# Both layer normalisations of a pair as ScalarE activations, the second one a slot later, in a software-pipelined two-layer transformer kernel

## What is computed

```
x = x + tanh(g_xattn[0]) * attention_0(layernorm(x), ctx)      16 heads of 8
x = x + tanh(g_ffn[0])   * experts_0(layernorm(x))             8 experts, one per token
x = x + tanh(g_xattn[1]) * attention_1(layernorm(x), ctx)
x = x + tanh(g_ffn[1])   * experts_1(layernorm(x))             8 experts, two per token
layernorm(x) = (x - mean) / sqrt(var + 1e-5)
```

## Time and profile before

| | |
|---|---|
| median of 3 runs | 875.13 us (874.2 to 876.31) |
| the profiled execution | 874.29 us, its span 872.5 us |
| TensorE, share of the span busy | 536.8 us, 62% |
| VectorE | 484.0 us, 55% |
| ScalarE | 349.5 us, 40% |
| GpSimd | 285.4 us, 33% |

### The profile page before, as it was taken

The page is one execution under the profiler, slowest core; times in us unless marked ns, Lnnn a source line. Parts: engine busy times, 40 slices in busy tenths (PEclk is TensorE's granted clock), DMA queues, the critical chain, the costliest instruction groups (busy, mean ns, idle before and its releaser), DMA issues.

```text
span 872.5 us, 16776 instructions
## 1 busy us (share of the span) xinstructions
PE 536.8 (62%) x5459; PEld 427.9 (49%) x5459; DVE 484.0 (55%) x1521; ACT 349.5 (40%) x795; POOL 285.4 (33%) x342
## 2 busy tenths in 40 slices
PE   1688999987200008862798999861000199999960
PEld 0566666664100007651566667640000199999960
DVE  4668888874588203434789999847200034444324
ACT  1157777766100004321266777762000055555530
POOL 6102222201001754771011111010777435555550
PEclk9979999999555559995699999995555599999995
DMA  7543333320000312325455553200311212222219
GB/s 251 151 136 88 87 88 88 88 58 2 0 0 3 101 55 81 106 77 137 124 144 148 158 153 97 59 2 2 101 53 52 62 53 73 75 71 75 74 37 288
DMA packets 94628, 76.37 MB, mean 88 GB/s; under 512 B 13904, under 2 KB 88528, under 8 KB 94096
## 3 DMA queue, kind: packets, MB, share of 16 engines
q1 hardware_dynamic: 86432, 57.05, 24.0%
q0 software_dynamic: 7040, 14.53, 4.9%
q10 hardware_dynamic: 1072, 3.73, 1.3%
HBM read 45.54 MB, written 33.46 MB: 91 GB/s over the span
## 4 chain that ended last, share of the span: by engine, by line
PE 41%; POOL 15%; DVE 12%; issue 10%; DMA 9%; ACT 7%; SPq 4%; ACTq 1%; DVEq 0%; POOLq 0%
POOL dispatched L407 10%; PE bank L730 8%; PE bank L740 8%; PE bank L683 6%; PE bank L577 4%; PE bank L551 4%; POOL returned L414 4%; PE bank L565 4%; DMA QS_N<-MH 3%; DVE PT L979 2%; DVE MX L789 2%; ACT N L496 2%; DMA returned<-PT,META_ROW 2%; ACT PT L443 2%; PE bank L630 1%
## 5 line engine op out<-in xcount | busy, mean ns | idle before, releaser
L789 DVE TENSOR_REDUCE MX<-bank 128x4 f32<-128x512 f32 x256 | 172.9, 685 | 45.0 <-PE bank L577 44.8
L443 ACT ACTIVATE PT<-bank 128x512 f32<-128x512 f32 x256 | 152.7, 600 | 107.2 <-PE bank L565 106.4
L414 POOL DMA_INDIRECT returned<-PT,META_ROW x124 | 119.1, 961 | 111.8 <-DVE PT L1070 87.1
L521 ACT ACTIVATE XGT<-bank 128x256 f32<-128x256 f32 x62 | 23.8, 384 | 260.3 <-PE bank L551 260.3
L551 PE MATMUL bank<-CONST,PT 128*128 128x128 f32 x124 | 25.9, 292 | 148.2 <-issue 142.1
L577 PE MATMUL bank<-KS,QS_N 96*128 96x128 f16 x1024 | 104.8, 229 | 12.1 <-DMA KS<-spread 10.0
L565 PE MATMUL bank<-QS_N,KS 98*128 98x512 f16 x256 | 99.2, 391 | 8.2 <-DMA QS_N<-MH 7.8
L740 PEld LDWEIGHTS bank<-WALL,HT 128*128 128x128 f32 x808 | 98.8, 192 | 10.2 <-issue 7.0
L740 PE MATMUL bank<-WALL,HT 128*128 x808 | 101.1, 276 | 3.9 <-issue 1.5
L730 PE MATMUL bank<-XGT,XT_HL_WR 128*128 128x256 f32 x404 | 100.7, 389 | 0.0
L577 PEld LDWEIGHTS bank<-KS,QS_N 96*128 96x128 f16 x1024 | 78.5, 104 | 34.1 <-DMA KS<-spread 11.6
(11 more groups left out here) (172 smaller groups left out, 830.5 us busy)
## 6 DMA issues: line engine op xcount, KB each, us to landing
spread<-XT_HL_WR SPq DMA_DIRECT2D x128, 64.0 KB, 2.1
PT<-dispatched SPq DMA_DIRECT2D x62, 130.0 KB, 2.1
QS_N<-spread SPq DMA_DIRECT2D x128, 48.0 KB
KS<-spread SPq DMA_DIRECT2D x32, 192.0 KB
WALL<-in_w SPq DMA_DIRECT2D x8, 578.0 KB, 4.0
CT<-in_ctx SPq DMA_DIRECT2D x32, 128.0 KB, 2.7
spread<-XT_HL_WR SPq DMA_DIRECT2D x32, 128.0 KB, 2.3
dispatched<-in_pads SPq DMA_DIRECT2D x2, 1040.0 KB, 5.7
```

The source lines that it names most:

```text
L414: pool.indirect_dma_start(ys[layer][:, :], bass.IndirectOffsetOnAxis(ap=META_ROW[:, a.f, c:c + 1], axis=0), YS[:, a.f, c, :], None).then_i ...
L443: nc.scalar.activation(PT[:, c, 4 * g:4 * g + 4, :].rearrange("p j q -> p (j q)"), ST[i % 2][:, :], ACT.Exp, scale=SCALE[layer]).then_inc( ...
L789: V.tensor_reduce(out=MX[:, m.u, 2 * J * g + c:2 * J * (g + 1):2], in_=MB[i % 2][:, :].rearrange("p (j k) -> p j k", j=J), op=ALU.max, axi ...
```

## The change

- The second normalisation of a pair (z, now y) and all that follows it move one slot later for ScalarE and TensorE: N is made at the start of ScalarE's slot, behind exponential 4 of b; its transposes stand in TensorE's group 2; NT is copied behind exponential 7 of b; the logits go to PF in place of PA in group 4; LG is copied behind exponential 1 of a.
- The first normalisation XN becomes two ScalarE activations with a scale and an offset, behind exponential 1 of a, in place of two VectorE instructions between maxima 6 and 7.
- The small terms (variance plus epsilon, minus the mean) leave VectorE. GpSimd makes them, for both normalisations: three instructions more for n, two more for z. GpSimd takes z after the bias of n.
- VectorE's slot is put in another order. Behind maximum 0: MH as before; behind 1: reciprocal and OK of z (before: at the slot's end, for b); behind 2: statistics of n; behind 5: the new x of z (before: 3); behind 6: the low half of f (before: 5); behind 7: statistics of z (before: 4).
- TensorE's slot: the transpose of the maxima comes before score block 4; XN's transposes move from group 1 to 0; the first half of the weighted sums from 0 to 1, the second from 4 to 5; OK's transposes from 0 to 2; Wo and the logits from 2 to 4; the value projection from 5 to 6; OT's transposes from 6 to 7; N's transposes from 7 to the next slot's 2.
- On ScalarE, XT goes from behind exponential 6 to behind 5, and OKT from behind 5 to behind 6.

```diff
@@ GpSimd, attention_slot
-                        nc.gpsimd.tensor_tensor(out=RSTD[:, n.u, :], in0=VE[:, n.u, :], in1=EXPO[:, :], op=ALU.pow).then_inc(x_rstd, 1)
...
+                        chain.link(nc.gpsimd.tensor_scalar(out=VE[:, n.u, :], in0=MV[:, n.u, :, 1], scalar1=LN_EPS, scalar2=None, op0=ALU.add))
+                        nc.gpsimd.tensor_scalar(out=MINUS_X[:, n.u, :], in0=MV[:, n.u, :, 0], scalar1=-1.0, scalar2=None, op0=ALU.mult)
+                        chain.link(nc.gpsimd.tensor_tensor(out=RSTD[:, n.u, :], in0=VE[:, n.u, :], in1=EXPO[:, :], op=ALU.pow))
+                        nc.gpsimd.tensor_tensor(out=OFFSET[:, n.u, :], in0=MINUS_X[:, n.u, :], in1=RSTD[:, n.u, :],
+                                                op=ALU.mult).then_inc(x_rstd, 1)
...
+                        nc.gpsimd.tensor_scalar(out=MINUS[:, z.u, :], in0=MV_N[:, z.u, :, 0], scalar1=-1.0, scalar2=None, op0=ALU.mult)
+                        chain.link(nc.gpsimd.tensor_scalar(out=VE_N[:, z.u, :], in0=MV_N[:, z.u, :, 1], scalar1=LN_EPS, scalar2=None, op0=ALU.add))
@@ ScalarE, attention_slot
                     exponentials(b, 4)
                     if y:
...
+                        act.wait_ge(n_rstd, y.g + 1)
+                        for c in range(2):
+                            last = nc.scalar.activation(N[:, y.b + c, 0:D], batch(y, c), ACT.Identity,
+                                                        scale=RSTD_N[:, y.u, c:c + 1], bias=OFFSET_N[:, y.u, c:c + 1])
+                        last.then_inc(n_copied, 1)
 
                     exponentials(b, 5)
+                    if f:
+                        act.wait_ge(front_t, f.g + 1)
+                        nc.scalar.activation(XT[:, f.u, :], PF[:, 0:256], ACT.Copy).then_inc(front_kept, 1)
...
                     exponentials(a, 1)
...
+                    if n:
+                        act.wait_ge(x_rstd, n.g + 1)
+                        act.wait_ge(front_t, before(n.g - 1))
+                        for c in range(2):
+                            last = nc.scalar.activation(XN[:, n.u, c * D:(c + 1) * D], batch(n, c), ACT.Identity,
+                                                        scale=RSTD[:, n.u, c:c + 1], bias=OFFSET[:, n.u, c:c + 1])
+                        last.then_inc(x_norm, 1)
@@ TensorE, attention_slot, group 2
+                    scores_for_maxima(2)
+                    scores(b, 6)
                     if z and layer == 0:
                         pe.wait_ge(o_kept, z.g + 1)
                         for c in range(2):
                             last = transpose(PO[:, c * P:(c + 1) * P], OK[:, c * D:(c + 1) * D])
                         last.then_inc(ok_t, 1)
...
+                    if y:
+                        pe.wait_ge(n_copied, y.g + 1)
                         if m:
                             pe.wait_ge(v_kept, m.g + 1)
...
+                        if f:
+                            pe.wait_ge(front_kept, f.g + 1)
+                        pe.wait_ge(lg_kept, y.g)
                         for c in range(2):
...
+                            last = transpose(PF[:, 256 + c * P:256 + (c + 1) * P], N[:, y.b + c, 0:D])
+                        last.then_inc(n_t, 1)
@@ VectorE, attention_slot
                     maxima(7)
...
+                    if z:
+                        dve.wait_ge(x_new, z.g + 1)
+                        dve.wait_ge(n_stats, z.g)
+                        dve.wait_ge(n_copied, before(z.g - 1))
+                        stats(z, STATS_N, MV_N[:, z.u]).then_inc(n_stats, 1)
```

More of the change, by code:

```diff
@@ L491, in slot @@
                                              ACT.Copy).then_inc(v_kept, 1)
[L493 to L498, removed]
                     exponentials(a, 3)
@@ L582, in slot @@
                     scores_for_maxima(0)
-                    scores(b, 4)
                     if a:
@@ L594, in slot @@
                         last.then_inc(ok_t, 1)
[L596 to L599, removed]
+                    if y:
+                        pe.wait_ge(n_copied, y.g + 1)
                         if m:
                             pe.wait_ge(v_kept, m.g + 1)
-                        if y:
-                            pe.wait_ge(n_kept, y.g + 1)
+                        if f:
+                            pe.wait_ge(front_kept, f.g + 1)
+                        pe.wait_ge(lg_kept, y.g)
                         for c in range(2):
[L605 to L621, removed]
+                            last = transpose(PF[:, 256 + c * P:256 + (c + 1) * P], N[:, y.b + c, 0:D])
+                        last.then_inc(n_t, 1)
                     scores_for_maxima(3)
@@ L635, in slot @@
                     scores(a, 0)
-                    if b:
+                    if z and layer == 0:
+                        pe.wait_ge(ok_kept, z.g + 1)
+                        for c in range(2):
+                            last = nc.tensor.matmul(PO[:, 256 + c * P:256 + (c + 1) * P], OKT[:, c * P:(c + 1) * P],
+                                                    WSQ[:, 3, :], start=True, stop=True)
+                        last.then_inc(wo_done, 1)
+                    if y:
+                        pe.wait_ge(n_kept, y.g + 1)
+                        for c in range(2):
+                            last = nc.tensor.matmul(PF[:, 256 + E * c:256 + E * c + E], NT[:, c * P:(c + 1) * P],
+                                                    WG[:, layer, :], start=True, stop=True)
+                        last.then_inc(lg_done, 1)
+                    scores_for_maxima(5)
+                    scores(a, 1)
+                    if b:
+                        values(b, 1)
+                    scores_for_maxima(6)
+                    scores(a, 2)
+                    if r:
+                        pe.wait_ge(front_kept, f.g + 1 if f else r.g + 1)
                         if y:
                             pe.wait_ge(lg_kept, y.g + 1)
-                        values(b, 1)
-                    scores_for_maxima(5)
-                    scores(a, 1)
-                    if r:
-                        pe.wait_ge(front_kept, f.g + 1 if f else r.g + 1)
                         pe.wait_ge(v_kept, r.g)
```

100 lines of the change are left out of this document (40 added, 60 removed).

## The result

| | before | after |
|---|---|---|
| median | 875.14 us (874.2 to 876.31, 4 runs) | 885.95 us (883.71 to 886.67, 4 runs) |
| profiled execution | 874.29 us, span 872.5 | 886.01 us, span 883.9 |

The account below looks back on a forecast made before the run. A ring of waits, no full engine, was taken to bound the kernel. Full slots -0.6 and +2.9, draining -2.1, -1.5, -1.9, -1.4, tail +0.4, filling -1.65 summed to -5.85 us: 869 predicted, range 861 to 881.

Parts of the forecast that it names:

- the ring: Loop from maximum 7 through statistics, GpSimd, N, XT, TensorE and back sets the slot: 10.77 us layer 0, 10.14 layer 1.
- its sign in layer 1: Layer 1's full slots get longer, 10.14 us against 9.85, adding 2.9 us over ten slots.
- signs of being wrong: Prediction fails if small GpSimd instructions cost over 0.5 us, TensorE stops elsewhere, or layer 1's slot is under 9.85 us.
- x: Unknown price of the two new small GpSimd instructions before the power of z, between 0.10 and 1.38 us.
- With x = 0.30: Path from the start of maximum 7 to N's transposes takes 4.55 us, with the small GpSimd pair at 0.30.
- x = 0.65: Alternative price of the GpSimd pair at twice VectorE's 0.16 us each; whole 7 us slower, about 876.
- TensorE wakes 0.05: TensorE starts N's transposes 0.05 us after ScalarE's XT copy ends.
- the ends: Filling and draining of the layers' pipelines make -8.55 us of the sum, its roughest part.
- Draining: Slots without pair f get shorter: -2.1 and -1.5 us; each layer's last two slots another -1.9 and -1.4.
- Filling: First XN 0.75 us later in layer 0; three slots without y gain some 0.4 us each per layer: -1.65.
- GpSimd makes it slower: Small pair before the power of z costs more; every 0.1 us adds 2 us over 20 slots; chance 0.22.
- the ends give little: Filling and draining bring a third of their -8.55 us; about 875, no change; chance 0.17.

Follow-up runs that it names:

- e6_xn_on_dve: Changed kernel with the first normalisation XN back on VectorE as two instructions behind maximum 4; ratio to the kernel before 1.0127, layer 0 slot 11.12 us.
- e1: Changed kernel with ScalarE's XT copy ahead of N instead of behind N and exponential 5; ratio to the kernel before 0.9909, layer 0 slot 10.24 us.
- e2: Changed kernel with VectorE's statistics of z right behind the new x instead of behind maximum 7; ratio to the kernel before 0.9862, layer 0 slot 10.04 us.
- e4: Changed kernel with the second normalisation's two small instructions ahead of the power back on VectorE; ratio to the kernel before 0.9998, layer 0 slot 10.78 us.
- e5: Changed kernel with two more small chained GpSimd instructions ahead of the power of z; ratio to the kernel before 1.0681, layer 0 slot 11.72 or 13.37 us.
- e7: Changed kernel with one semaphore wait instead of four before TensorE's transposes of N; ratio to the kernel before 1.0058, layer 0 slot 10.94 us.
- e8_filler: Changed kernel with two groups of two throwaway TensorE matmuls in the draining slots of both layers; ratio to the kernel before 1.0137, layer 1 drain 39.95 us.
- e12_filler_l1: Changed kernel with throwaway TensorE matmuls in layer 1's draining slots alone; ratio to the kernel before 1.0077, layer 1 drain 39.96 us.
- e14_both_terms: Changed kernel with z's small pair back on VectorE and one wait before N's transposes; ratio to the kernel before 0.9963, layer 0 slot 10.61 us.
- b0: The kernel before, unedited, profiled again on a chip of the experiments; layer 0 slot 10.85 us, layer 1 drain 38.88 us.
- e0: The changed kernel, unedited, run again as control; ratio to the kernel before 1.0096, layer 0 slot 11.12 us, layer 1 drain 42.19 us.

## Why the prediction was wrong

**Right: the ring, its members and its sign in layer 1.** ScalarE idle about 1 us before N, released by OFFSET_N (1.18); TensorE stopped by XT and by maximum 7, and no stop for OKT or OT; XN covered on ScalarE (e6_xn_on_dve). e1, e2, e4, e5 and e7 each changed one member, and the slot of layer 0 followed within 0.1 us where the clock stayed up. One of my signs of being wrong did appear, a stop of TensorE elsewhere (0.35 us for OK), but it doesn't set the slot.

**Wrong by size: x.** The step "With x = 0.30": the pair costs 0.51 us (0.59 less one wake of 0.08), since the second one starts 0.29 us behind the first and the power 0.30 behind that. It neither overlaps fully nor costs a power. This is 0.21 us of a slot. My estimate of x = 0.65 by the Trainium skill, GPSIMD Engine Reference, section 4.1, misread it: the factor of about two is stated there for two-input operations, while one-input operations, as both of the pair are (a tile and a constant), run at roughly line rate. Here one of them lasts 0.22 to 0.23 us against VectorE's 0.16: more than that, and less than twice. What counted is the distance of the starts, 0.29 and 0.30 us, and not the duration; that the pair's 0.51 lies nearer to 0.65 than to my 0.30 is chance.

**Wrong by size: "TensorE wakes 0.05".** I took it from a place where the first of four waits ends last. Here the third does, and the transposes start 0.26 us behind XT; with one wait it is 0.05 (e7_one_wait). The Trainium skill, Perfetto Trace Analysis, Identifying Dependency Chains, says that an instruction that waits on several engines may have extra semaphore instructions ahead of it. That would make room for such a cost, but it doesn't say why four waits cost 0.05 us in one order and 0.26 in another, and no run here shows those instructions apart. This is 0.21 us of a slot. Of the two, 0.42 us, the slot shows 0.35: 10.77 forecast and 11.12 measured, 10.14 and 10.49; the other terms were together 0.07 too large.

**Wrong: the ends.** e4_small_on_dve happens to have the very ring that I had forecast (10.78 and 10.14), and yet its ratio is 0.9998, not the 0.993 of my 869. So even with the ring right, 869 would have missed, by about 6 us. The step "Draining" failed in layer 1 (-2.7 forecast, +4.0 measured). I had put the clock there at nothing. Of these 6.7 us, it is at least 2.2 to 2.7 (e8_filler, e12_filler_l1). The two ring terms lie in the draining slots and the tail too; without them and with the clock up, drain 1 is 37.38 (e14_both_terms), 1.5 us below the kernel before (38.88 in b0). Even that is 1.2 us short of the forecast of -2.7, so "Draining" was too hopeful by itself as well. A wait for MH's transfer may be part of it, but no run tests this:

```profile
564.62 0.61 PE L579 MATMUL bank<-QS_N,KS 98*128 98x512 f16 x1 [0.83 <-DMA QS_N<-MH]
```

In layer 0 the same step had -3.8 and got -2.2; without that fall of the clock at 209.7 it is -3.2 (41.50 in e0 against 44.65 in b0). "Filling" failed by 1.8 us in layer 0: the first MH is 0.55 us later (40.36 against 39.81), about as forecast, but the three slots behind it lose 0.8 us where I had them gain 1.2. There the first score block waits 2.88 us for MH's transfer, 1.32 before; no run separates why. Part of it doesn't come back in the second pair of traces: up to the MH of pair 3 the changed kernel is 0.4 us later there (74.77 in e0, 74.39 in b0) and not 1.3.

**The rivals.** "GpSimd makes it slower" named the place and the price per 0.1 us (2 us) rightly; the pair and the wake had 0.42 us too little. The ends went further than in "the ends give little": together they cost about 2 us, where I had them give 8.15. I had given each its chance as if they excluded each other; together they are the result. None of my cases had the clock in it, since it stood at 1.00 in the earlier trace rows. Yet in the same trace it is at the lower level for 10.2 us behind 40.9 and for 3.3 us behind 58.0, while the pipeline of layer 0 fills, so it does fall in an attention stage outside the full slots.

## What to carry to other kernels

When work is moved a slot later to save a round trip, look for the loop that this closes: here statistics behind the last maximum, and the result wanted early in the next slot. Put each member of a loop as early as its inputs allow, and keep the copy that others wait for (XT) ahead of the one that comes late (N); these two moves turned 1.0% slower into 1.8% faster, while moving XN between the engines in the same order did nothing. On TensorE, drop waits that a later wait on the same engine already implies, look which of several waits ends last, and count a stop at more than its length, since the clock may fall behind it.

## What the runs showed of the hardware

- **A wait among four.** TensorE started 0.26 us behind the event when it belonged to the third of four waits, and 0.05 us behind it when it belonged to the first of four (kernel before; e1_xt_first, layer 1) or to the only one (e7_one_wait).
- **Small GpSimd instructions.** A 128x2 instruction with a constant lasts 0.22 us, but two independent ones in a row start 0.29 us apart, and a chained one 0.30 us behind the last start.
- **TensorE's clock behind a stop.** With a stop of 0.69 us in each slot the clock stayed at 2.4 GHz in all of layer 0's full slots; with 1.29 us it fell to 1.2 GHz in six of ten, and the slot shown lost 1.65 us by it. Two throwaway matmuls ahead of each stop in layer 1's drain kept it up there and gave back 2.2 to 2.7 us; in layer 0's drain they cost 3.2. Yet layer 1's full slots have stops of up to 1.5 us at full clock, so the length of a single stop doesn't decide it. What does is not settled here.
